# Widening a channel dimension with float32 matmuls on quarters of the array in place of split float16 ones

## What is computed

```python
h = jnp.einsum('oc,bchw->bohw', w_in, x)              # 64 -> 256 channels
f = jnp.fft.rfft2(patches_8x8(h)) * fft_filt
h = from_patches(jnp.fft.irfft2(f, s=(8, 8)))
h = lax.conv_general_dilated(h, w_dw, (1, 1), 'SAME', feature_group_count=c)
x1, x2 = jnp.split(h, 2, axis=1)
g = jax.nn.gelu(x1, approximate=False) * x2
return jnp.einsum('oc,bchw->bohw', w_out, g)          # 128 -> 64 channels
```

## Time and profile before

| | us |
|---|---|
| median of 3 runs (5405.21 to 5406.29) | 5405.63 |
| the profiled execution | 5406.3 |
| its span, from the first instruction to the last | 5404.5 |

### The profile page before, as it was taken

One profiled execution on the slowest core, in us unless ns is written; L12 is line 12 of the kernel. 1 busy time (PEld: TensorE's weight loads), 2 busy tenths in 40 slices (PEclk: granted clock), 3 DMA queues, 4 the chain that ended last, 5 costly groups with the idle time before them and its releaser, 6 DMA issues.

```text
span 5404.5 us, 201429 instructions
## 1 busy us (share of the span) xinstructions
PE 5202.6 (96%) x88868; PEld 3195.1 (59%) x88868; DVE 4642.3 (86%) x5703; ACT 3739.5 (69%) x4866; POOL 4643.1 (86%) x2727
## 2 busy tenths in 40 slices
PE   5999999999999999999999999999999999999998
PEld 4565655656556565565656556565665655656554
DVE  6889888888888888888898888988889888888876
ACT  3766767677676766767767676676766767677675
POOL 3889889898888988889888898888989889898898
PEclk9999999999999999999999999999999999999999
DMA  2011110110101111010010101101011110110000
GB/s 103 19 50 42 38 44 29 53 40 37 54 22 50 40 40 53 19 57 36 36 53 32 48 33 39 54 36 43 33 50 40 40 42 31 50 43 20 23 26 26
DMA packets 43953, 219.31 MB, mean 41 GB/s; under 512 B 5366, under 2 KB 6104, under 8 KB 36952
## 3 DMA queue, kind: packets, MB, share of 16 engines
q1 hardware_dynamic: 43096, 206.42, 9.9%
HBM read 103.64 MB, written 102.76 MB: 38 GB/s over the span
## 4 chain that ended last, share of the span: by engine, by line
PE 69%; DVE 15%; POOL 7%; issue 5%; ACT 3%; DMA 0%; DVEq 0%; SPq 0%; POOLq 0%; ACTq 0%
PE PS L953 20%; PE PS L971 17%; PE PS L912 14%; PE PS L941 10%; POOL v_lo L357 6%; DVE v L697 5%; PE PS L985 5%; DVE hf L690 4%; DVE g L722 2%; PE PS L921 2%; ACT v_hi L487 2%; DVE bn L628 2%; DVE PS L713 1%; ACT carry L516 1%; POOL xf_lo L351 0%
## 5 line engine op out<-in xcount | busy, mean ns | idle before, releaser
L357 POOL TENSOR_TENSOR v_lo<-v,v_hi 128x1024 f16<-128x1024 f32 (+1 forms) x1792 | 3354.6, 1898 | 455.4 <-ACT v_hi L487 455.0
L697 DVE TENSOR_TENSOR v<-PS,smul 128x1024 f32<-128x1024 f32 (+1 forms) x1792 | 1910.4, 1086 | 361.6 <-POOL v_lo L357 200.9
L487 ACT ACTIVATE v_hi<-v 128x1024 f16<-128x1024 f32 (+1 forms) x1792 | 1646.8, 944 | 717.5 <-DVE v L697 561.9
L953 PE MATMUL PS<-hf,c_nodes 64*64 64x512 f32 (+1 forms) x14336 | 1659.7, 556 | 70.4 <-DVE v L697 57.0
L971 PEld LDWEIGHTS PS<-c_ext,v_hi 128*128 128x128 f16 x14336 | 1129.9, 97 | 507.2 <-ACT carry L511 165.0
L971 PE MATMUL PS<-c_ext,v_hi 128*128 128x100 f16 (+2 forms) x14336 | 1258.9, 203 | 9.7 <-issue 4.1
L971 PE MATMUL PS<-c_ext,v_lo 128*128 128x100 f16 (+2 forms) x14336 | 1250.6, 202 | 0.0
L971 PEld LDWEIGHTS PS<-c_ext,v_lo 128*128 128x128 f16 x14336 | 1118.2, 97 | 1.2
L690 DVE TENSOR_TENSOR hf<-PS,mult 128x1024 f32<-128x1024 f32 (+1 forms) x896 | 954.8, 1086 | 86.7 <-PE PS L941 66.2
L953 PEld LDWEIGHTS PS<-hf,c_nodes 64*64 64x64 f32 x14336 | 406.8, 131 | 623.1 <-DVE v L697 219.7
L912 PE MATMUL PS<-S_hi,csign 64*64 64x448 f16 (+2 forms) x8640 | 746.8, 336 | 9.4 <-POOL S_lo L346 9.4
(11 more groups left out here) (74 smaller groups left out, 5846.0 us busy)
## 6 DMA issues: line engine op xcount, KB each, us to landing
out_x<-Xa SPq DMA_DIRECT2D x96, 448.0 KB, 2.5
out_x<-Xb SPq DMA_DIRECT2D x96, 448.0 KB, 2.5
Xa<-in_x SPq DMA_DIRECT2D x8, 2240.0 KB, 9.0
Xb<-in_x SPq DMA_DIRECT2D x8, 2240.0 KB, 8.9
Xa<-in_x SPq DMA_DIRECT2D x8, 1792.0 KB, 7.7
Xb<-in_x SPq DMA_DIRECT2D x8, 1792.0 KB, 6.8
Xa<-in_x SPq DMA_DIRECT2D x8, 1344.0 KB, 5.9
Xb<-in_x SPq DMA_DIRECT2D x8, 1344.0 KB, 6.7
```

The source lines that it names most:

```text
L357: nc.gpsimd.tensor_tensor(v_lo[:, img, :, k0:k1, :], v32[:, V_BUF[kind(b, s)][img][grp], :, 0:k1 - k0, :], v_hi[:, img, :, k0:k1, :], ALU. ...
L487: nc.scalar.activation(v_hi[:, img, :, k0:k1, :], v32[:, V_BUF[kind(b, s)][img][grp], :, 0:k1 - k0, :], ACT.Copy).then_inc(act_vhi[img], 1)
L697: nc.vector.tensor_tensor(v32[:, V_BUF[kind(b, s)][img][grp], :, 0:k1 - k0, :], PS[:, bank:bank + 2, 0:(k1 - k0) * C2].rearrange("p i (k c ...
L953: last = nc.tensor.matmul(PS[points, bank + side, 0:(k1 - k0) * C2], c_nodes[half, points], hf[half, img, k0:k1, :].rearrange("p k c -> p ...
```

## The change

Widening is done in float32, as `forward_transform` and `evaluated` are: for each block four matmuls of 256 columns, one on each quarter of the array (64 rows for an image, 64 columns for a patch). The float16 parts xf_hi, xf_lo, win_hi and win_lo are gone, and with them one ScalarE and one GpSimd instruction in every step and two VectorE instructions at the start. Widening waits for ScalarE's copy of the spectrum (`act_xf`), and the next strip's `pixels` waits for all four widening groups of the strip before (`pe_hf`).

```diff
@@ GpSimd
-            def spectrum_low(n, s):
-                pool.wait_ge(act_xh, n * STRIPS + s + 1)
-                nc.gpsimd.tensor_tensor(xf_lo[:], xf[:], xf_hi[:], ALU.subtract).then_inc(pool_xl, 1)
@@ ScalarE
             def pixels(n, s, bank):
                 act.wait_ge(pe_xT, n * STRIPS + s + 1)
                 if n or s:
-                    act.wait_ge(pool_xl, n * STRIPS + s)
+                    act.wait_ge(pe_hf, 4 * (n * STRIPS + s))
...
-            def spectrum_high(n, s):
-                i = n * STRIPS + s
-                act.wait_ge(act_xf, i + 1)
-                if i:
-                    act.wait_ge(pe_hf, 4 * i)
-                nc.scalar.activation(xf_hi[:], xf[:], ACT.Copy).then_inc(act_xh, 1)
@@ VectorE
-            nc.vector.tensor_copy(win_hi[:], win_sb).then_inc(dve_prep, 1)
-            dve.wait_ge(dve_prep, 3)
-            nc.vector.tensor_tensor(win_lo[:], win_sb, win_hi[:], ALU.subtract).then_inc(dve_prep, 1)
@@ TensorE
             def widened(b, s, grp, bank):
                 k0, k1 = GROUPS[grp]
-                pe.wait_ge(pool_xl, b * STRIPS + s + 1)
+                pe.wait_ge(act_xf, b * STRIPS + s + 1)
                 for k in range(k0, k1):
-                    for part, (xf, win) in enumerate(((xf_hi, win_hi), (xf_lo, win_hi), (xf_hi, win_lo), (xf_lo, win_lo))):
-                        for r in range(IMGS):
-                            last = nc.tensor.matmul(PS[:, bank + r, (k - k0) * C2:(k - k0 + 1) * C2],
-                                                    xf[r * C:(r + 1) * C, k, :], win[r * C:(r + 1) * C, :],
-                                                    start=part == 0, stop=part == 3)
+                    for r, side in ((0, 0), (1, 1), (0, 1), (1, 0)):
+                        last = nc.tensor.matmul(PS[side * P * P:(side + 1) * P * P, bank + r, (k - k0) * C2:(k - k0 + 1) * C2],
+                                                xf[r * C:(r + 1) * C, k, side * P * P:(side + 1) * P * P],
+                                                win_sb[r * C:(r + 1) * C, :], start=True, stop=True)
                 last.then_inc(pe_hf, 1)
```

More of the change, by code:

```diff
@@ L146, in build @@
         alpha_sb = sb("alpha_sb", [128, 1])
-        win_hi = sb("win_hi", [128, C2], F16)
-        win_lo = sb("win_lo", [128, C2], F16)
+        win_sb = sb("win_sb", [128, C2])
         wout_sb = sb("wout_sb", [HC, C])
@@ L160, in build @@
         xf = xT
-        xf_hi = sb("xf_hi", [128, NBLK, BPX], F16)
-        xf_lo = sb("xf_lo", [128, NBLK, BPX], F16)
         hf = sb("hf", [BPX, IMGS, NBLK, C2])
@@ L187, in build @@
         filt_sb = v32[0:NF, 0, 1, 0, :]
-        win_sb = v32[:, 2, 0, 0, :]
         c_taps = v32[0:9, 0, 0, 1, 0:128]
@@ L227, in build @@
         dve_conv = sem("dve_conv")
-        pool_xl = sem("pool_xl")
-        act_xh = sem("act_xh")
         dve_hf = sem("dve_hf")
@@ L295, in _ @@
                              (c_nodes[:], nodes), (c_taps, taps), (ext32, ext), (filt_sb, filt), (wdw_sb, w_dw),
-                             (wout_sb[:], w_out), (win_sb[0:C], w_in), (win_sb[C:128], w_in)):
+                             (wout_sb[:], w_out), (win_sb[0:C, :], w_in), (win_sb[C:128, :], w_in)):
                 sp.dma_start(dst, src).then_inc(dma_const, 16)
@@ L385, in image @@
                             low_nodes(mid[0], mid[1], 0, 2)
-                        if front:
-                            spectrum_low(n, t)
                         if mid:
@@ L554, in image @@
                             spectrum(n, t, BANK_P)
-                            spectrum_high(n, t)
                         if mid:
@@ L1218, in _ @@
             groups_x(0)
-            pe.wait_ge(dve_prep, 6)
+            pe.wait_ge(dve_prep, 4)
             for j in range(STRIPS):
```

## The result

The changed kernel took 5431.6 us (5429.9 to 5433.1, 4 runs), the kernel before, run beside it, 5405.4 us: a ratio of 1.0049, 95% interval 1.0037 to 1.0061. It is slower by 26 us. It is slower, as forecast, and inside the stated range (5394 to 5440 us), but outside the forecast's own 5408 to 5425 us: the value was 16 us short, and most of what follows is about these 16 us.

A forecast was written before the change was run, and what follows sets the result against it. TensorE, busy for 96%, was taken to bound the kernel, with plain-step chains also crossing VectorE, ScalarE and GpSimd. 5406.3 - 4.2 (start) + 14.3 (groups) = 5416.4 us, stated as 5416 after a 0.7 us median adjustment; range 5394 to 5440 us.

The forecast's parts named there:

- The relief at nothing: Removing xf_hi on ScalarE and xf_lo on GpSimd was costed at nothing in 222 of 224 steps.
- relief counts: Rival, chance 0.17: GpSimd paces a step, 1.85 us back once per image, 5372 or 5386 us; in half the images, 5401.
- The start: Start of the pipeline: removed instructions and a wait in the second strip give -4.2 us (-3.5 to -4.9).
- The new waits: Widening waiting for xf, and ScalarE's next pixel copy waiting for the last widening, were both forecast to cost nothing.
- The length of a group: Each widening group longer by its head: +0.035 us for one block, +0.04 for two (bounds -0.01 to +0.06).
- how much of it is on the path: Group growth reaching the chain: 0.075 us per convolution or last-image step, 0.05 per other plain step, together +14.3 us.
- Loads seen at every block: Rival, chance 0.11: each two-block widening group shows its weight-load head once more, 34 us on top, 5450 us.

## Why the prediction was right, and by how much it was short

**The relief at nothing** held nearly: put back as dead work it costs nothing, taken away alone it gives 5 us, 3 in the first two steps and 2 in plain steps later on. The rival "relief counts", 1.85 us back in half or all of the images, is out.

**The start** was forecast at -4.2 us and gave about -3.4: widening begins 3.0 us earlier after the transform and the first two strips take 3.2 us less between them, but the first transform starts only 0.25 us earlier. The parts of w_in were 0.63 us of the chain, and I named only the widening as late next; late next at that place were TensorE's group sums, 1.0 us, which had been hidden beneath them.

**The new waits** cost nothing, as argued: ScalarE waited for the transposes for 638.9 us before and for 646.0 us after, and no wait of L450 (pixels) for widening stands among the waits.

**The length of a group** was right for the one-block group (0.48 us) and for a two-block group ahead of L944: w1 starts at 2629.42 and L944 at 2630.45,

```profile
2629.42 1.09 PE L914 MATMUL PS<-win_sb,xT 64*64 64x256 f32 x16
2630.45 0.22 PE L944 MATMUL PS<-c_ext,v_hi 128*128 128x100 f16 x1
```

1.03 us against 0.98 before. It comes from the head, as the prediction had it: the first set of quarters takes 0.27 us to the next and each later one 0.22, where a float16 pair took 0.12 and then 0.11. The load times that it named for this, 93 and 131 ns, differ by type and by tile at once; with the type kept, 93 becomes 105 ns on quarters.

**What was mis-sized** is "how much of it is on the path". Two terms of it failed. For w2 before the projection I had added nothing; it starts behind a wait, shows its head like the others, and costs 0.05 us (0.98 to 1.02 us to the projection). And for w3 I had passed on the growth of its own length, 0.035 us, where what counts is how long after w3's start VectorE's product can begin: 0.73 - 0.66 = 0.07 us. Why that grows by twice as much as the length is not shown. A convolution step therefore grew by 0.16 us and not by 0.075 (105 steps: 17 us, 8 forecast). The plain steps pay the way to VectorE on both w3 and w0. For w0 the chain of the earlier trace rows hides it, since L971 stands between; the timelines show L953 (now L926) waiting for the product of w0 and starting 2.37 us behind w0 before, 2.44 after:

```profile
5340.56 0.28 PE L941 MATMUL PS<-win_hi,xf_hi 64*128 64x256 f16 x2 [0.39 <-DVE hf L690]
...
5342.93 1.52 PE L953 MATMUL PS<-hf,c_nodes 64*64 64x256 f32 x16
```

```profile
5366.47 1.09 PE L914 MATMUL PS<-win_sb,xT 64*64 64x256 f32 x16 [0.34 <-DVE hf L667]
...
5368.91 1.52 PE L926 MATMUL PS<-hf,c_nodes 64*64 64x256 f32 x16
```

A step of the last image grew from 20.57 to about 20.72 us, twice the 0.075 forecast, and the other plain steps grew by 0.10 us in the mean (0.06 to 0.17) where I had 0.05: 2 and 11 us, 6 forecast. 17 + 11 + 2 - 3.4 is 27 us; the spans of the two profiled executions differ by 26.3. That they agree to a microsecond is partly chance, as now and then a single step differs by 1 us and more from one execution to another.

**The bounds and the range.** The bounds of this term failed too. I had set 0.06 us on a group and two groups a step on the path, 27 us in all; w3 and w0 cost 0.07 us by their way to VectorE, a convolution step has three groups on the path, and the groups together cost 30 us. With the start, these bounds end at 5429 us, below the 5431.6 measured. The result lies in the stated range only because that had been drawn up to 5440 us for another reason, loads seen at every block, which did not happen. So the mechanism was right in kind, a longer head of each group; its price on the path was put at 14 us and measured at 30; and that the range held is luck. I had taken the value from the length of a group and not from its way to VectorE.

**Loads seen at every block** is out as well. Inside a group a block follows the one before it after 0.43 us, as long as in float16 (0.44), and a two-block group grew by 0.05 us, one head and not two. The rule of the Trainium skill that a weight load overlaps running matmuls only where its row group differs ("TensorE: Matmul & The Clock Gate", "The mechanism") would have given 5830 us; the trace disagrees with it, since 56 loads of 132 ns a step in sets of four run beneath matmuls of the same row groups. The same section of the Trainium skill also lets a load run ahead where it goes to the background weight buffer, which the prediction left out; whether it is that here, no run shows.

## What to carry to other kernels

An engine that is busy for 86% of the time and stands on the chain need not give back more than a few microseconds when it is relieved: look at what it waited for just before the instruction that counts, and put the work back as dead work to be sure. A group of matmuls costs by two numbers, from its start to the next work on TensorE and from its start to the engine that reads its result; where they alternate with another engine it is the second, and equal array time says nothing about either. What helped here was the order of two instructions on the engine that the waiting one waited for.

## What the runs showed of the hardware that I had not expected

A weight load of 64 rows took 93 ns in float16 for 128 columns and 105 ns for 64, the wider one being the faster; in float32 132 ns for 64 columns and 186 ns for 128. A float32 matmul of 256 columns cost the same array time on a half as on a quarter, 0.43 us a block once a group runs, so that the half, with half as many instructions, lost only by its head (0.54 us from w3 to w0 in place of 0.48). And passing from quarters to halves between two groups, or back, cost about 0.1 us, as did passing from quarters to the whole array.
